# Spreading a block's rounds of weight sums over its attention units, and mixing one quarter later

## The chip, the cores and the metric

The kernel runs on one core of a Trainium2 chip. The metric is the time of one execution on the device in microseconds (us); the median of several runs counts. The core's engines work side by side, each through its own list of instructions in order: TensorE (PE, with its weight loads PEld), VectorE (DVE), ScalarE (ACT), GpSimd (POOL) and SyncE (SP). They wait for one another through semaphores.

## The reference, cut to what matters

2048 tokens (32 sequences of 64, 1024 wide) pass a grouped attention and a linear layer with adapters. All is float32.

```python
mixed = einsum('bct,bcd->bdt', x, W_mix[itok])        # one 64x64 matrix per sequence: "mixing"
q, k, v = mixed @ Wq.T, mixed @ Wk.T, mixed @ Wv.T    # 32 heads of 128 for q, 8 for k and v
q, k = rmsnorm(q) * q_norm_w, rmsnorm(k) * k_norm_w
attn = softmax(q @ k.T / sqrt(128) + alibi_bias)      # causal, 64x64 per sequence and head
x = x + (attn @ v) @ Wo.T                             # output projection
x = x + ffn(base_and_low_rank(x))                     # linear in x, folded into one 1024x1024 matrix
```

## The kernel before

**Tiling.** The tokens are worked in four blocks of 512, each of four tiles of 128 tokens. A block is a list of units: `kv` (keys and values of two key heads), `q` (queries of one key head's four heads, with their attention), `o` and `p` (output projection of a pair of key heads) and `f` (the last linear layer, two halves). `units()` gives the order: kv q q kv o q q kv o q q kv o q q p o f f. A kv, q or f unit has four steps, one for each tile; a step is four **quarters**, each of six 128x512 matmuls (each product is made of three, of the upper and lower parts of both factors, so that float32 is kept). A block has 336 quarters. In block 0 the first pair of q units spans quarters 16 to 48, the first projection `o` 64 to 92, the next two q units 92 to 124, the second projection 140 to 168, the q units behind it 168 to 200, the third projection 216 to 236.

**The order.** It is written out by `Order` before the program is built. `at(base, delay, work)` puts work at a position in quarters; `tick` steps from quarter to quarter and takes all work whose position has been reached, in order of position. Every engine then goes through the same list and takes its own stages. Delays of stages behind a step stand in `AT`; those of the keys' transposes in `KEYS_AT` (transpose on PE, k_hi on ACT, k_lo on DVE), where "mixing" is for the first three steps of a block's first kv unit in blocks 1 to 3. A q step runs: four quarters of matmuls, square (ACT), mean (DVE), rstd (POOL), scale (DVE), query_t (PE), q_hi (ACT), q_lo (DVE), scores (PE), alibied, biased, peak (DVE), exp (ACT), total, inverse, prob (DVE), transpose (PE), p_hi, p_twice (ACT), p_lo (DVE), the product with the values (PE).

**Weights.** Each quarter's weights are loaded by SP into one of four raw buffers; w_hi (ACT) and w_lo (DVE, 128x1024) split them into one of six slots of a ring, when the slot's former chunk is done. So four w_lo come together at the end of a kv or q unit: at 30.6, 32.6, 33.6 and 35.6 for the unit that ends at quarter 32, and at the same places of the other units.

**Weights' sums.** The projection is done by seven products of sums instead of eight (`OPS`), so it needs four sums of the quarters of `Wo` for each of eight rounds (pair, c). A round (`sums_load`, `sums_add`, `sums_store`) is four t_load of 512 KB on POOL, four additions t1 to t4 of 128x1024 on DVE (7.2, 8.7, 10.2 and 11.7 quarters after the round's start) and four t_store on POOL (at 12.8), into `t_scratch`, from where later units fetch them as weights through SP. Three rounds run in the setup, five in block 0 at `ROUND_AT`. Their buffers lie in `lefts`, the left factors of the projections; so each round has to be done before a projection in block 0 needs them (`ROUND_BEFORE`, a wait in op_hi), and a round must not start while one runs.

**Mixing.** `f_step` of the second f unit loads the next block's tile of x (`reload`, on POOL), splits it (`mix_split`: x_hi on ACT, x_lo on DVE) and mixes it (`mix`: 16 matmuls into four banks, four a_hi on ACT, four a_rest and four a_lo on DVE, written as act_lo). The tile at step i of the f unit ends its step at quarter 324 + 4i of its block, and is needed by the next block's first kv unit at quarter 336 + 4i.

Of the kernel before, what the change touches and what calls it, by code (L numbers as in the profile page):

```python
# [19 lines left out]
HEADS, KV_HEADS, HD = 32, 8, 128  # L20
# [25 lines left out]
          tp=7.9, tp_hi=8, tp_again=9.2, tp_lo=8.6,  # L46
          v=10.6, v_hi=11.5,
          add=1.6,
          mix_split=7.4, mix=9.8, reload=5.1,
          x1=2.2, low=4.6, low_end=6.0, out=0.6, c22=0.2,  # L50
          w_hi=0.3, w_lo=0.9)

KEYS_AT = dict(mixing=(2.8, 3.4, 3.9), queries=(3.8, 4.4, 4.9), projection=(4.8, 5.4, 5.9))
LATE = dict(s=0.5, s_add=0.5, s_exp=0.5, s_norm=0.5, tp=1.2, tp_hi=1.2, tp_again=1.2, tp_lo=1.2, v=1.6, v_hi=1.6)


# [5 lines left out]
OPS = (("11", "11", "a"), ("s3", "t3", "d"), ("12", "21", "a"), ("s2", "t2", "b"),  # L65
       ("s1", "t1", "e"), ("22", "t4", "b"), ("s4", "22", "e"))
# [10 lines left out]
QUARTERS = 4  # L77
# [7 lines left out]
SETUP_ROUNDS = 3  # L85

WARM = 22, 8
ROUND_AT = (0.5, 18.5, 35, 104, 180)

ROUND_BEFORE = (2, 1), (3, 0), (3, 1), (3, 1)  # L90

PART_OF = [(n + 2) % TILES for n in range(KT + 1)]

# [13 lines left out]
def ops_of(unit):  # L107


    kind, blk, pair = unit  # L110
    if kind == "p":
        return 4, 6
    return (0, 1, 2, 3, 5) if pair == 2 else range(len(OPS))


def tiles_of(blk):

    return (0, 1, 2, 3) if blk % 2 == 0 else (2, 3, 0, 1)


def is_o(unit):
    return unit[0] in ("o", "p")
# [71 lines left out]
class Order(Plan):  # L194
# [249 lines left out]
    def blocks(self):  # L444

        self.at(0, 14, lambda: self.add("fx_store"))
        for n in range(SLOTS, len(self.chunks)):
            self.at(self.prepared_at[n], 0, self.prepare)
        for (pair, c), start in zip(ROUNDS[SETUP_ROUNDS:], ROUND_AT):
            self.at(start, 0, lambda pair=pair, c=c: self.sums_load(pair, c))  # L450

            wait = 3.5 if start < QUARTERS else 0
            for i, stage in enumerate(("t1", "t2", "t3", "t4")):
                self.at(start, wait + 7.2 + 1.5 * i, lambda pair=pair, c=c, stage=stage: self.sums_add(pair, c, [stage]))
            self.at(start, wait + 12.8, lambda pair=pair, c=c: self.sums_store(pair, c))
        for u, unit in enumerate(self.units):
            if unit[0] == "o":
                self.left_factors(unit)
            elif unit[0] == "p":

                for tp in range(2):
                    self.at(QUARTERS * self.first_step[unit], tp - 2.9, lambda unit=unit, tp=tp: self.kept_sum(unit[1], unit[2], tp))
        for k, (u, i) in enumerate(self.steps):
            kind, blk, n = self.units[u]
            if k in (0, 1):
                self.later(FIRST_MIX[k], lambda k=k: self.mix(0, k + 2))
            if kind == "kv":
                self.kv_step(k)
            elif kind == "q":
                self.q_step(k, n, tiles_of(blk)[i])  # L470
            elif is_o(self.units[u]):
                self.o_step(k, blk, n, ops_of(self.units[u])[i])
            else:
                self.f_step(k, blk, n, tiles_of(blk + 1)[i])
        while self.side:
            self.tick()
# [44 lines left out]
    def kv_step(self, k):  # L521
# [7 lines left out]
        else:  # L529
            place = "projection" if i == TILES - 1 else "queries"  # L530
        transposed, upper, lower = KEYS_AT[place]

# [191 lines left out]
def build_program(nc, d, out):  # L724
# [3 lines left out]
    with ctx:  # L728
# [193 lines left out]
        def o_step(blk, pair, m):  # L922
            return order.op[blk, pair, m]
# [321 lines left out]
        def _(eng):  # L1245
# [10 lines left out]
            for stage, key in order.stages:  # L1256
# [180 lines left out]
                elif stage == "op_hi":  # L1437
# [12 lines left out]
                    if blk == 0:  # L1450
                        for i in range(4):
                            w.wait_ge(f"t_store{i}", *ROUND_BEFORE[pair])
                    w.wait_ge("mix_mm", blk, tiles_of(blk)[2], len(MIX_BANKS) - 1)
# [363 lines left out]
        @block.gpsimd  # L1817
        def _(eng):
            w = Waits(eng, order, done)
            for stage, key in order.stages:  # L1820
                if stage == "mixw_zero":
                    eng.memset(mixw_raw[:, :, :], 0.0).then_inc(done[stage], 1)
                elif stage == "half_set":
                    eng.memset(half[:, :], -0.5).then_inc(done[stage], 1)
                elif stage == "ones_set":
                    eng.memset(prob[:, :], 1.0).then_inc(done[stage], 1)
                elif stage.startswith("f_store"):
                    n, u = key
                    w.wait_ge("f_copy", n, u)
                    eng.dma_start(f_scratch[u, n // 2, :, n % 2, :], stage_tile(order.copies[n, u][0])).then_inc(done[stage], 16)  # L1830
                elif stage in ("x0", "x1", "x2", "x3"):
                    blk, = key
                    t = int(stage[1])
                    if blk > 0:
                        w.wait_ge(f"out{t}", blk - 1)
                    elif t < 2:
                        left, of = order.first_tiles[t]
                        w.wait_ge(left, *of)
                    else:
                        for left, of in order.stage_left:  # L1840
                            w.wait_ge(left, *of)
                    eng.dma_start(acc[:, t, :], d["x"][blk * TILES + t]).then_inc(done[stage], 16)
                elif stage == "rstd":
                    k, = key
                    heads = norm_width(k)
                    w.wait_ge("mean", k)
                    w.wait_ge("half_set")
                    if earlier_norm(k, 1) is not None:
                        w.wait_ge("scale", earlier_norm(k, 1))
                    eng.tensor_tensor(rstd[:, 0:heads], mean[:, 0:heads], half[:, 0:heads], ALU.pow).then_inc(done[stage], 1)  # L1850
                elif stage.startswith("t_load"):
                    pair, c = key
                    i = int(stage[-1])
                    n = ROUNDS.index(key)
                    if n == 0:
                        w.wait_ge("coef_masked")
                    elif n == SETUP_ROUNDS:

                        w.wait_ge("weff_mm", KT, 1, 3)
                        w.wait_ge("w_hi", SLOTS - 1)  # L1860
                    else:
                        w.wait_ge(f"t_store{i}", *ROUNDS[n - 1])
                    if pair == KV_HEADS // 2 - 1:
                        w.wait_ge("mm", o_step(0, c, len(OPS) - 1), 3)
                    eng.dma_start(sums_of(pair, c)[i][:, :], d["wo"][pair, i, c]).then_inc(done[stage], 16)
                elif stage.startswith("t_store"):
                    pair, c = key
                    i = int(stage[-1])
                    name = next(t for t in SUM_AT if SUM_AT[t] == i)
                    w.wait_ge(name, pair, c)  # L1870
                    eng.dma_start(t_scratch[pair, int(name[1]) - 1, c], sums_of(pair, c)[i][:, :]).then_inc(done[stage], 16)
                elif stage in ("fx_load0", "fx_load1"):
                    blk, = key
                    i = 2 * int(stage[-1])
                    last = KV_HEADS // 2 - 1
                    w.wait_ge("fx_store")
                    w.wait_ge("s4", blk, last)
                    w.wait_ge("op_lo", o_step(blk, last, 4 if i == 0 else 6))
                    eng.dma_start(extra[:, i:i + 2, :], extra_scratch[:, i:i + 2, :]).then_inc(done[stage], 16)
                elif stage == "biased_x":  # L1880
                    blk, t = key
                    w.wait_ge("a_lo", "x1", blk, t | 1, 1)
                    w.wait_ge("bias_add", 1)
                    eng.tensor_tensor(acc[:, t, :], acc[:, t, :], bias_eff[:, :], ALU.add).then_inc(done[stage], 1)
                elif stage.startswith("out"):
                    blk, = key
                    t = int(stage[3])
                    f_k = order.first_step["f", blk, 1] + tiles_of(blk + 1).index(t)
                    w.wait_ge("acc", f_k, 1)
                    eng.dma_start(out[blk * TILES + t], acc[:, t, :]).then_inc(done[stage], 16)  # L1890
            for t in range(TILES):
                w.wait_ge(f"out{t}", BLOCKS - 1)
            for left, of in order.stage_left:
                w.wait_ge(left, *of)
            eng.memset(half[:, :], -0.5).then_inc(done["half_set"], 1)
# [92 lines left out]
```

## Time and profile before

| | us |
|---|---|
| Median of three runs (lowest, highest) | 2375.29 (2374.58, 2379.8) |
| Profiled execution, own time | 2375.95 |
| its span | 2374.0 |
| PE busy | 2344.8 |
| DVE busy | 1776.3 |
| ACT busy | 1464.5 |
| POOL busy | 285.1 |

The main loop starts 136.6 us after the span's start and ends at 2360.1; what stands ahead of it is the setup. Busy PE is counted from modelled ends of pipelined matmuls, so a wait shorter than a matmul's tail doesn't show as idle time; the distance from the start of one group of matmuls to the next shows it. "Granted clock" is the share of TensorE's full clock that the chip grants.

### The profile page before, as it was taken

The numbers are of one execution on the slowest core, as the hardware profiler recorded it, in microseconds if no ns is written. First come the engines' busy times: TensorE is split into PE (matmuls) and PEld (weight loads), VectorE is DVE, ScalarE is ACT, GpSimd is POOL, SyncE is SP. The second block draws the span as 40 slices with busy tenths as digits, with TensorE's granted clock in tenths as the row PEclk, the third lists the DMA queues.
The fourth block names the chain that finished last, engine by engine and source line by source line (L and its number), as shares of the span: only waits on it lengthen the run. The fifth ranks groups of instructions, "written<-read, shape, count | busy, mean of one in ns | idle before, by whom it ended". The sixth has DMA issues, their size and how long they took to land.

```text
span 2374.0 us, 33429 instructions
## 1 busy us (share of the span) xinstructions
PE 2344.8 (99%) x11706; PEld 1961.6 (83%) x11706; DVE 1776.3 (75%) x2930; ACT 1464.5 (62%) x3625; POOL 285.1 (12%) x336
## 2 busy tenths in 40 slices
PE   8999999999999999999999999999999999999998
PEld 6877888888888888888888888888888888888886
DVE  6777969696847878787846777777876696969691
ACT  4246767576625857576824857576844676767660
POOL 1222010101011001010021101010021101010111
PEclk9999999999999999999999999999999999999999
DMA  6774434442542242423443242423244242423250
GB/s 254 265 262 187 160 134 155 147 135 73 195 150 89 86 145 74 148 72 134 143 153 116 72 160 71 160 72 124 97 172 144 81 150 70 151 80 139 73 197 36
DMA packets 88440, 316.16 MB, mean 133 GB/s; under 512 B 12716, under 2 KB 13228, under 8 KB 87124
## 3 DMA queue, kind: packets, MB, share of 16 engines
q1 hardware_dynamic: 70292, 247.14, 30.1%
q0 software_dynamic: 16256, 62.92, 7.2%
q10 hardware_dynamic: 1728, 3.98, 0.5%
q8 instruction: 95, 1.56, 0.3%
q14 instruction: 69, 0.57, 0.1%
HBM read 282.54 MB, written 31.46 MB: 132 GB/s over the span
## 4 chain that ended last, share of the span: by engine, by line
PE 94%; DVE 3%; DMA 1%; issue 1%; ACT 0%; POOL 0%; ACTq 0%; POOLq 0%; DVEq 0%
PE main L1041 80%; PE qt_bank L1202 3%; PE s_bank L1218 3%; PE s_bank L1219 2%; PE pv_bank L1239 1%; PE pv_bank L1238 1%; PE pt_bank L1226 1%; PE pt_bank L1041 1%; DVE ring L1511 1%; DVE setup L1511 0%; PE qt_bank L1139 0%; PE s_bank L1139 0%; DMA acc<-in_x 0%; DMA t_scratch<-sums 0%; DMA mask<-in_masks 0%
## 5 line engine op out<-in xcount | busy, mean ns | idle before, releaser
L1041 PE MATMUL main<-ring,act_hi 128*128 128x512 f32 x3584 | 1148.4, 402 | 0.4 <-DVE ring L1511 0.3
L1041 PEld LDWEIGHTS main<-ring,act_hi 128*128 128x128 f32 x3584 | 641.5, 189 | 114.3 <-issue 3.1
L1041 PE MATMUL main<-ring,act_lo 128*128 128x512 f32 x1792 | 701.7, 392 | 0.0
L1041 PE MATMUL main<-ring,lefts 128*128 128x512 f32 x2688 | 625.9, 391 | 0.0
L1041 PEld LDWEIGHTS main<-ring,lefts 128*128 128x128 f32 x2688 | 499.9, 188 | 101.5
L1511 DVE TENSOR_TENSOR ring<-raw,ring 128x1024 fp32r<-128x1024 f32 x448 | 550.5, 1233 | 41.1 <-ACT ring L1249 38.9
L1249 ACT ACTIVATE ring<-raw 128x1024 fp32r<-128x1024 f32 x448 | 472.0, 1056 | 172.0 <-PE main L1041 149.6
L1041 PEld LDWEIGHTS main<-ring,act_lo 128*128 128x128 f32 x1792 | 336.9, 188 | 74.9
L1850 POOL TENSOR_TENSOR rstd<-mean,half 128x4 f32<-128x4 f32 (+1 forms) x192 | 174.0, 906 | 1535.1 <-DVE mean L1636 1535.0
L1382 ACT ACTIVATE sq<-main 128x128 f32<-128x128 f32 x640 | 169.3, 277 | 76.1 <-PE main L1041 72.2
L1410 ACT ACTIVATE prob<-score,peak 128x64 f32<-128x64 f32 x512 | 136.1, 336 | 98.1 <-DVE peak L1694 97.4
L1514 DVE TENSOR_TENSOR acc<-main,acc 128x512 f32<-128x512 f32 x164 | 112.2, 685 | 87.2 <-PE main L1041 87.1
L1249 ACT ACTIVATE qt_hi<-qt_bank 128x512 fp32r<-128x512 f32 x128 | 76.6, 598 | 126.8 <-PE qt_bank L1202 124.9
L1715 DVE TENSOR_TENSOR pt_lo<-pt_bank,pt_hi 64x256 fp32r<-64x256 f32 x256 | 107.7, 421 | 59.2 <-ACT pt_hi L1420 57.5
L1420 ACT ACTIVATE pt_hi<-pt_bank 64x256 fp32r<-64x256 f32 x256 | 96.9, 379 | 66.8 <-PE pt_bank L1226 65.3
L1511 DVE TENSOR_TENSOR lefts<-quads,lefts 128x1024 fp32r<-128x1024 f32 x112 | 136.5, 1219 | 0.5
L1249 ACT ACTIVATE lefts<-quads 128x1024 fp32r<-128x1024 f32 x112 | 118.3, 1056 | 25.9 <-PE main L1041 23.4
L1656 DVE TENSOR_TENSOR qn<-main,rstd 128x512 f32<-128x512 f32 (+1 forms) x192 | 114.5, 596 | 25.7 <-POOL rstd L1850 24.2
L1382 ACT ACTIVATION_READ_ACCUMULATOR sq<-main 128x1 f32 x640 | 131.6, 206 | 0.0
L1511 DVE TENSOR_TENSOR qt_lo<-qt_bank,qt_hi 128x512 fp32r<-128x512 f32 x128 | 88.0, 688 | 57.4 <-ACT qt_hi L1249 57.4
L1219 PE MATMUL s_bank<-k_t,qt_lo 128*128 128x64 f32 x512 | 117.3, 245 | 0.0
L1218 PE MATMUL s_bank<-k_t,qt_hi 128*128 128x128 f32 x512 | 115.1, 286 | 1.2 <-issue 1.2
(168 smaller groups left out, 2554.3 us busy)
## 6 DMA issues: line engine op xcount, KB each, us to landing
raw<-in_wq SPq DMA_DIRECT2D x128, 512.0 KB, 4.3
raw<-t_scratch SPq DMA_DIRECT2D x128, 512.0 KB, 3.2
raw<-in_wo SPq DMA_DIRECT2D x96, 512.0 KB, 3.2
raw<-in_wkv SPq DMA_DIRECT2D x64, 512.0 KB, 3.9
sums<-in_wo POOLq DMA_DIRECT2D x32, 512.0 KB, 7.6
t_scratch<-sums POOLq DMA_DIRECT2D x32, 512.0 KB, 4.1
raw<-f_scratch SPq DMA_DIRECT2D x32, 512.0 KB, 4.9
acc<-in_x POOLq DMA_DIRECT2D x16, 512.0 KB, 4.1
```

What stands on the lines that cost most here:

```text
L1041: mm = eng.matmul(bank, a, b, start=start and n == 0 and m == 0, stop=stop and n == len(terms) - 1 and m == 2, skip_group_check=further)
L1218: eng.matmul(s_bank[:, a:a + 2 * SEQ], lh, keys, start=True, stop=False)
L1219: mm = eng.matmul(s_bank[:, a:a + SEQ], ll, keys[:, 0:SEQ], start=False, stop=True)
L1249: eng.activation(dst, src, ACT.Copy).then_inc(done[stage], 1)
L1382: act = eng.activation(sq[:, tile(h)], norm_bank(k)[:, tile(h)], ACT.Square, accum_out=ssum[:, h:h + 1])
L1410: act = eng.activation(prob[:, cols], score[:, cols], ACT.Exp, bias=peak[:, r:r + 1], scale=-1.0)
L1420: act = eng.activation(pt_hi[rows_of(b), b, :], pt_bank[rows_of(b), 0:256], ACT.Copy)
L1511: eng.tensor_tensor(dst, src, f32(upper), ALU.subtract).then_inc(done[stage], 1)
L1514: eng.tensor_tensor(dst, a, b, ALU.add).then_inc(done[stage], 1)
L1656: eng.tensor_tensor(heads_of(norm_tile(k)[:, cols], heads), heads_of(norm_bank(k)[:, cols], heads), along(rstd[:, 0:heads], heads), ALU.mu ...
L1715: rest = eng.tensor_tensor(pt_lo[rows_of(b), b, :], pt_bank[rows_of(b), 0:256], f32(pt_hi[rows_of(b), b, :]), ALU.subtract)
L1850: eng.tensor_tensor(rstd[:, 0:heads], mean[:, 0:heads], half[:, 0:heads], ALU.pow).then_inc(done[stage], 1)
```

## The change

Five things are edited. The five rounds of block 0 start at 24, 95, 111.5, 171 and 187.5 quarters instead of 0.5, 18.5, 35, 104 and 180. `ROUND_BEFORE` follows: the first projection waits for round (1,1), the second for (2,1), the third and fourth for (3,1). The extra 3.5 quarters that the round of the first quarters had are dropped. The t_loads of both rounds of pair 2 and of pair 3 wait for the end of the projection two pairs earlier (0 or 1); before, only those of pair 3 waited, each for another projection. And at the edges of blocks the split moves from 7.4 to 8.4 and the mixing from 9.8 to 10.5, with the keys of the "mixing" steps from 2.8, 3.4, 3.9 to 3.8, 4.35, 4.38.

```diff
@@ AT
-          mix_split=7.4, mix=9.8, reload=5.1,
+          mix_split=8.4, mix=10.5, reload=5.1,
@@
-KEYS_AT = dict(mixing=(2.8, 3.4, 3.9), queries=(3.8, 4.4, 4.9), projection=(4.8, 5.4, 5.9))
+KEYS_AT = dict(mixing=(3.8, 4.35, 4.38), queries=(3.8, 4.4, 4.9), projection=(4.8, 5.4, 5.9))
@@
-ROUND_AT = (0.5, 18.5, 35, 104, 180)
-
-ROUND_BEFORE = (2, 1), (3, 0), (3, 1), (3, 1)
+ROUND_AT = (24, 95, 111.5, 171, 187.5)
+
+ROUND_BEFORE = (1, 1), (2, 1), (3, 1), (3, 1)
@@ blocks
             self.at(start, 0, lambda pair=pair, c=c: self.sums_load(pair, c))
-
-            wait = 3.5 if start < QUARTERS else 0
             for i, stage in enumerate(("t1", "t2", "t3", "t4")):
-                self.at(start, wait + 7.2 + 1.5 * i, lambda pair=pair, c=c, stage=stage: self.sums_add(pair, c, [stage]))
-            self.at(start, wait + 12.8, lambda pair=pair, c=c: self.sums_store(pair, c))
+                self.at(start, 7.2 + 1.5 * i, lambda pair=pair, c=c, stage=stage: self.sums_add(pair, c, [stage]))
+            self.at(start, 12.8, lambda pair=pair, c=c: self.sums_store(pair, c))
@@ gpsimd, t_load
-                    if pair == KV_HEADS // 2 - 1:
-                        w.wait_ge("mm", o_step(0, c, len(OPS) - 1), 3)
+                    if pair >= 2:
+                        w.wait_ge("mm", o_step(0, pair - 2, len(OPS) - 1), 3)
```

## Rows read from the trace of the kernel before

**Rows 1.** The page: busy time of PE, and the chain by engine

```profile
PE 2344.8 (99%) x11706; PEld 1961.6 (83%) x11706; DVE 1776.3 (75%) x2930; ACT 1464.5 (62%) x3625; POOL 285.1 (12%) x336
...
PE 94%; DVE 3%; DMA 1%; issue 1%; ACT 0%; POOL 0%; ACTq 0%; POOLq 0%; DVEq 0%
```

**Rows 2.** Windows: stretch, length, busy by engine (instructions), granted clock, DMA share, GB/s

```profile
136.60:703.20 566.60, 557.59 (x2776) 464.55 (x2777) 435.71 (x715) 358.40 (x894) 79.93 (x100) 0.99 0.44 158
703.20:1256.40 553.20, 553.20 (x2794) 465.23 (x2793) 418.30 (x702) 356.50 (x893) 60.29 (x62) 1.00 0.35 119
...
136.60:153.50 16.90, 15.99 (x82) 12.88 (x83) 15.95 (x27) 10.76 (x22) 2.82 (x5) 1.00 0.88 314
```

**Rows 3.** Timeline, second tile of block 2: start us, us, instruction; PE, then DVE

```profile
1259.09 0.28 PE L1125 MATMUL qt_bank<-mixw,x_odd 128*128 128x256 f32 x1
...
1260.88 0.68 PE L1041 MATMUL main<-ring,act_hi 128*128 128x512 f32 x2
...
1262.32 0.62 PE L1041 MATMUL main<-ring,act_hi 128*128 128x512 f32 x2
...
1263.81 0.70 PE L1041 MATMUL main<-ring,act_hi 128*128 128x512 f32 x2
...
1263.24 0.43 DVE L1514 TENSOR_TENSOR act_lo<-pv_bank,act_lo 128x256 fp32r<-128x256 f32 x1
```

**Rows 4.** PE's waits in blocks 1 to 3 (total, times, longest); ACT's timeline, block 2

```profile
PE qt_bank L1125 <- DVE k_t L1511: 0.7, 1, 0.7
...
1272.33 1.06 ACT L1249 ACTIVATE x_odd<-acc 128x1024 fp32r<-128x1024 f32 x1 [3.34 <-DMA acc<-in_x]
```

**Rows 5.** PE's waits in block 0: total us, times, longest

```profile
PE qt_bank L1202 <- DVE qn L1656: 6.0, 4, 4.1
...
PE qt_bank L1202 <- DVE qn L1663: 0.7, 1, 0.7
```

**Rows 6.** POOL's timeline around its wait; landing of all t_stores (source view, L1871)

```profile
167.02 1.06 POOL L1871 DMA_DIRECT2D t_scratch<-sums  x2 [1.16 <-DVE sums L1775]
...
177.67 0.53 POOL L1865 DMA_DIRECT2D sums<-in_wo  x1 [3.54 <-DMA t_scratch<-sums]
178.22 1.04 POOL L1850 TENSOR_TENSOR rstd<-mean,half 128x4 f32<-128x4 f32 x1
...
DMA to landing us min/median/max: 3.0/4.1/9.8
```

**Rows 7.** Windows, columns as in rows 2, behind that wait

```profile
178.60:185.40 6.80, 5.36 (x15) 4.39 (x16) 1.55 (x3) 1.74 (x9) 0.88 (x2) 0.50 0.69 281
```

**Rows 8.** Timeline at the round of quarter 35: DVE, then PE

```profile
231.34 1.22 DVE L1775 TENSOR_TENSOR sums<-sums,sums 128x1024 f32<-128x1024 f32 x1
232.48 0.68 DVE L1511 TENSOR_TENSOR qt_lo<-qt_bank,qt_hi 128x512 fp32r<-128x512 f32 x1
...
229.00 0.60 PE L1202 MATMUL qt_bank<-ident,qn 128*128 128x128 f32 x4
...
233.26 0.30 PE L1218 MATMUL s_bank<-k_t,qt_hi 128*128 128x128 f32 x1 [0.66 <-issue]
...
238.42 0.66 PE L1202 MATMUL qt_bank<-ident,qn 128*128 128x128 f32 x4 [0.79 <-DVE qn L1656]
```

**Rows 9.** PE timeline, same place of block 1, without a round

```profile
755.86 0.60 PE L1202 MATMUL qt_bank<-ident,qn 128*128 128x128 f32 x4
...
759.29 0.22 PE L1218 MATMUL s_bank<-k_t,qt_hi 128*128 128x128 f32 x1
...
763.53 0.66 PE L1202 MATMUL qt_bank<-ident,qn 128*128 128x128 f32 x4
```

**Rows 10.** Timeline, first tile of block 2: PE, then DVE

```profile
1251.09 0.28 PE L1125 MATMUL qt_bank<-mixw,lefts 128*128 128x256 f32 x1
...
1252.11 0.42 DVE L1511 TENSOR_TENSOR act_lo<-qt_bank,act_hi 128x256 fp32r<-128x256 f32 x1 [2.85 <-ACT act_hi L1249]
...
1254.94 0.42 DVE L1514 TENSOR_TENSOR act_lo<-pv_bank,act_lo 128x256 fp32r<-128x256 f32 x1
```

## The prediction

> **What bounds the kernel now.** I read the page's busy shares and its chain first: TensorE (PE) is busy 99% of the span and carries 94% of the chain [rows 1]. PE runs one written-out order of 1344 quarters (six 128x512 matmuls each; 1.36 us from start to start in the median), so time is lost only where PE waits in that order. Next I cut the trace at the first matmul of each block of tokens [rows 2]: block 0 takes 566.6 us, block 1 takes 553.2. Block 0 also mixes one tile less (1.79 us, 1259.09 to 1260.88 [rows 3]), so it loses 15.2 us that block 1 doesn't. Its first eight quarters with two mixings lose 2.2 of them: 16.9 us [rows 2] against 8 x 1.36 + 2 x 1.8 + 0.14 for a transpose = 14.7; nothing that the change moves stands there for PE. The other 13.0 us are, as far as the trace tells, what the rounds of weights' sums cost. Blocks 1 to 3 have no round, and one PE wait of note, 0.7 us, with some 0.5 behind it [rows 4]. So there are 13 us to win from in block 0, and 1.2 us at the block edges.
>
> **Part 1: where the 13 us sit.** Round (2,0) follows round (1,1) too soon. Its t_loads wait on GpSimd (POOL) for the t_stores of the round before, POOL takes its work in order, and behind them stands rstd, which scale and query_t need. POOL waits 3.54 us for the last store, issues the load at 177.67 and rstd only at 178.22 [rows 6]. PE waits 4.1 us for that scale [rows 5], and the granted clock then is 0.50 for 6.8 us [rows 7]; PE restarts at 180.0, so 5.4 us run at half rate, 2.7 us more. With 0.7 us for the key transpose behind the round's additions [rows 5], that is 7.5 us. The other 5.5 are VectorE's (DVE's) backlog at the five rounds.
>
> **The change removes that POOL wait.** Round (1,1) starts at 24 with no store just ahead of it. Rounds (2,0) and (3,0), at 95 and 171, wait for a projection that ends at quarter 92 or 168, and POOL's next rstd is due at 97.3 and 173.3. Rounds (2,1) and (3,1) start 16.5 quarters after their forerunners. From stores to the rstd behind the loads that leaves 5.5 quarters (107.8 to 113.3), 10.5 us at the 1.92 us that a quarter takes here (755.86 to 763.53 are four [rows 9]); a store lands 4.1 us after its issue in the median and 9.8 at most [rows 6]. Before, it was 4.5 short quarters (16.8 to 21.3), 6 to 7 us. So I cost the wait at nothing, at most 1 us. The five rounds still issue the same 20 loads, 20 stores and 20 additions; on SP nothing moves, since the results are fetched a projection later.
>
> **What the rounds cost on DVE in their new places.** Each addition takes a slot of 1.14 us on DVE (231.34 to 232.48 [rows 8]), in a stretch where four w_lo of the next weights take as much each within five quarters. The round at 35 shows the price. t4 stands ahead of q_lo, and the scores start at 233.26; the next query_t, behind its scale, at 238.42 [rows 8]. Without a round, query_t to scores takes 3.43 us and scores to query_t 4.24 [rows 9]; from the query_t at 229.00 the scores would come at 232.43, and the next query_t 4.24 after 233.26, at 237.50. So 0.83 + 0.92 = 1.8 us. t1 to t3 fall into gaps of DVE.
> - 95 and 171 stand at the same place of their unit (3 quarters in) as 35: 1.8 each.
> - 111.5 and 187.5 are half a quarter further on: t3 falls ahead of a scale (0.5), t4 ahead of q_lo (0.6), and the backlog reaches the next scale (0.9): 2.0 each.
> - 24 is the worst place. Its additions stand at 31.2, 32.7, 34.2, 35.7 and the w_lo at 30.6, 32.6, 33.6, 35.6. Laid into block 1's order [rows 9] at 1.14 us each: the scores come 0.2 late, the next query_t 2.1 (two additions ahead of its scale), the transpose of the probabilities 0.1, the next scores 1.4 (t3 and t4 ahead of q_lo): 3.8 us.
>
> Sum 1.8 + 1.8 + 2.0 + 2.0 + 3.8 = 11.4 us against 13.0: part 1 **gains 1.6 us**. Bounds: with each round at 0.8 (all but the last of its slots hidden) a gain of 9; with a half clock at the first round a loss of 1.
>
> On the clock, the rows show a fall after 4.1 us of waiting [rows 5, 7] and none after 0.8 [rows 8]. The Trainium skill, "TensorE: Matmul & The Clock Gate", section on the HAM clock gate, says that idleness of PE throttles the array to half (here 2.4 to 1.2 GHz) and activity frees it. The trace agrees; if the rule already takes the waits of 2.1 and 1.4 us at round (1,1) for idleness, the sum is that of the first rival below.
>
> **Part 2: the mixing.** An action at a position that is no whole quarter is taken at the next whole one. A mixing at 9.8 goes into PE's order two quarters ahead of the step that needs its tile; at 10.5 only one. So all 12 mixings for blocks 1 to 3 move by a whole quarter, not 0.7. Behind a mixing hangs a chain that can't shrink: four act_hi on ScalarE (ACT), eight act_lo on DVE, and the kv step's first matmul waits for the last of them. At the second tile of block 2 the mixing starts at 1259.09, the next quarters at 1260.88 and 1262.32, the step that needs the tile at 1263.81; its last act_lo starts at 1263.24 and takes 0.43, so PE starts 0.14 behind it [rows 3]: **the slack is already nil**. The chain by itself: the first act_lo 1.02 us after the mixing starts, the last ends at 1255.37, 4.28 us after it [rows 10]. One quarter later, PE has 1.79 (mixing) + 1.44 (one quarter) = 3.23 us of work from the mixing's start; it then waits 4.28 + 0.14 - 3.23 = 1.19, less 0.13 that it waits now (1262.32 to 1263.81 is 1.49, a quarter 1.36): **1.06 us a tile**. For the third and fourth tile a key transpose (0.14) fills some of it: 1.0 each. The first tile's cover is a quarter of nine matmuls (1.5 x 1.36 + 0.08 = 2.12, the 0.08 for following a mixing: 1.44 less 1.36): 4.42 - 3.91 = 0.5. One block edge: 0.5 + 1.06 + 1.0 + 1.0 = 3.6 us; three edges 10.8. The later split (8.4) and keys (3.8) don't lengthen the chain: laid out the same way, x_lo, mean, v_lo, scale and gain are through DVE before each chain's first act_lo, by 0.1 to 0.6 us. Where they are not, a tile costs up to 1.5.
>
> **What it gives back.** In block 2 the last tile's mixing waits on k_lo, since x_hi, held up 3.34 us by a late x tile, stands ahead of k_hi on ACT [rows 4]. With k_hi at 4.35 ahead of the split at 4.4, this goes: 1.2 us. Bounds of part 2: a loss of 8 to 14, less 1.2.
>
> **Sum.** -1.6 + 10.8 - 1.2 = +8.0 us. The profiled execution took 2375.95 us with a span of 2374.0, 0.7 us over the median of 2375.29; such a difference is noise, and I add to the median: **2383.3 us**, 0.34% slower.
>
> **Rivals.**
> - *The clock falls at round (1,1)*, after waits of 2.1 and 1.4 us within 7: another 2.7 us, 2386.0. 8%.
> - *The new places are nearly free*: all 13 us go but for 5 x 0.8, so -9.0 + 9.6 = +0.6: 2375.9, no change. For it: t1 to t3 of the round at 35 are free. Against: the w_lo stand just there, and the same count of slots reproduces the 1.8 us measured at 35. 10%.
> - *Faster: the kv step doesn't wait for the chain.* If the last act_lo came within 3.23 us of the mixing's start rather than 4.28, the later mixing would be hidden: -1.6 - 1.2, 2372.5, and 2365 if the new places are cheap as well. Against: eight DVE operations without a gap fill 3.26 us alone (1252.11 to 1255.37 [rows 10]), and 0.14 us between act_lo and matmul [rows 3] is a wait that just ended. 4%.
> - *The move is less than I read* (positions rounded otherwise): mixings cost half or nothing, 2373 to 2379. 4%.
>
> **How the numbers follow.** Forecast 74%: 2383.3. What a measurement can tell from no change is about 0.2%, 4.75 us: faster is under 2370.5, slower over 2380.0. The clock's rival is slower; the forecast is slower but for its lower end (cheaper rounds, about a tenth of it, with little lost at the edges); the cheap places and the smaller move are mostly same; the faster rival is shared between same and faster. Faster 0.03, same 0.15, slower 0.82. For 8 in 10 the range takes the forecast with its bounds and the clock's rival: 2378 to 2389.
>
> **What would show it.** Right: no POOL wait for t_scratch that holds an rstd, clock 1.00 through block 0, a query_t near quarter 34 that waits about 2 us for its scale, and at each block edge PE waits of about 1 us for act_lo ahead of kv steps. Wrong: kv steps that start on time after a mixing one quarter later; a first round without its wait of 2 us, or with a half clock; or new waits for t_scratch, x tiles or weights.

## The result, and the profile after

| | before | changed |
|---|---|---|
| median of six runs each, us (lowest to highest) | 2376.61 (2374.58 to 2379.8) | 2386.01 (2385.59 to 2386.99) |
| ratio of the runs' times (95% interval) | | 1.0039 (1.0026 to 1.0052) |
| span of the profiled execution, us | 2374.0 | 2384.4 |

The change costs 9.4 us by the medians and 10.4 us by the two profiled spans. The forecast was 2383.3 with a range of 2378 to 2389, and slower at 0.82. The new runs of the kernel before put its median 1.3 us above the one the forecast was added to; so the forecast rise of 8.0 us stands against 9.4 and 10.4. The spans are those of one profiled execution each, and the runs of the kernel before range over 5.2 us, those of the changed kernel over 1.4.

The page of the changed kernel, busy time of the engines and the chain by engine (compare [rows 1]):

```profile
PE 2345.0 (98%) x11706; PEld 1960.6 (82%) x11706; DVE 1772.8 (74%) x2930; ACT 1465.1 (61%) x3625; POOL 285.2 (12%) x336
...
PE 91%; DVE 6%; issue 1%; ACT 1%; DMA 0%; POOL 0%; ACTq 0%; POOLq 0%; DVEq 0%
```

The instructions and PE's busy time are the same; the chain has moved from PE (94% to 91%) to DVE (3% to 6%). PE stands still more, and what it stands still for is DVE.

The blocks, as windows of the changed kernel (stretch, length, busy by engine, granted clock, DMA share, GB/s; compare [rows 2]):

```profile
136.30:700.50 564.20, 554.64 (x2777) 462.84 (x2777) 435.08 (x715) 357.75 (x894) 80.08 (x100) 1.00 0.46 158
700.50:1258.70 558.20, 554.31 (x2793) 465.07 (x2793) 416.31 (x702) 356.63 (x894) 60.30 (x62) 1.00 0.36 118
1258.70:1816.90 558.20, 554.33 (x2792) 465.06 (x2793) 416.42 (x702) 356.69 (x894) 60.22 (x62) 1.00 0.36 118
1816.90:2370.40 553.50, 550.01 (x2768) 461.85 (x2769) 411.14 (x689) 348.02 (x882) 58.70 (x59) 1.00 0.33 110
```

Block 0 went from 566.6 to 564.2 us, and its clock from 0.99 to 1.00; block 1 from 553.2 to 558.2. Blocks 2 and 3 took 554.4 and 549.3 before. So the differences are -2.4, +5.0, +3.8 and +4.2 us, with -0.3 for the setup: 10.3 of the span's 10.4. The first tile's loss at the first edge (some 0.6 us) falls ahead of the cut, into block 0, so the rounds, all in block 0, gained about 3; the edges of blocks lost a lot.

The waits of PE in blocks 1 to 3 of the changed kernel (total us, times, longest):

```profile
PE main L1039 <- DVE act_lo L1512: 7.9, 9, 1.0
PE qt_bank L1200 <- DVE qn L1661: 2.6, 3, 0.9
PE main L1039 <- issue: 1.2, 3, 0.4
```

Before, only 0.7 us of waiting stood out there [rows 4]. The nine waits for act_lo are the second to fourth tile of each of three edges, and the three called "issue" the first tiles: these twelve were forecast. The three waits for qn, one at each edge, were not.

**The edge, seen closely.** The second tile of block 2, PE and then DVE (start us, us; idle time ahead of it in brackets), answers to [rows 3]:

```profile
1262.90 0.28 PE L1123 MATMUL qt_bank<-mixw,x_odd 128*128 128x256 f32 x1
...
1264.69 0.68 PE L1039 MATMUL main<-ring,act_hi 128*128 128x512 f32 x2
...
1267.32 0.47 PE L1039 MATMUL main<-ring,act_hi 128*128 128x512 f32 x1 [1.02 <-DVE act_lo L1512]
...
1266.75 0.42 DVE L1512 TENSOR_TENSOR act_lo<-pv_bank,act_lo 128x256 fp32r<-128x256 f32 x1
```

Now only one quarter lies between the mixing and the step that needs its tile. From that quarter's start to the step's it is 1267.32 - 1264.69 = 2.63 us; a quarter there takes 1.44, and 0.13 was waited before, so the tile costs 2.63 - 1.44 - 0.13 = 1.06 us.

**The wait for the store is gone.** POOL's timeline at the stores of round (2,0), the one at 95, and the loads of round (2,1):

```profile
318.12 1.06 POOL L1869 DMA_DIRECT2D t_scratch<-sums  x2 [3.98 <-DVE sums L1773]
...
324.00 0.53 POOL L1863 DMA_DIRECT2D sums<-in_wo  x1 [0.74 <-DMA t_scratch<-sums]
...
328.21 1.03 POOL L1848 TENSOR_TENSOR rstd<-mean,half 128x4 f32<-128x4 f32 x1 [3.69 <-DVE mean L1634]
```

A load still waits 0.74 us for its store (1.1 at the other such place), but POOL is idle again for 3.69 us before the next rstd asks for it. In [rows 6] the rstd came right behind the load.

**The round at 24.** PE, with DVE under it:

```profile
192.23 0.30 PE L1216 MATMUL s_bank<-k_t,qt_hi 128*128 128x128 f32 x1
...
198.52 0.66 PE L1200 MATMUL qt_bank<-ident,qn 128*128 128x128 f32 x4 [1.92 <-DVE qn L1654]
...
203.57 0.30 PE L1216 MATMUL s_bank<-k_t,qt_hi 128*128 128x128 f32 x1 [1.09 <-issue]
...
190.31 1.22 DVE L1762 TENSOR_TENSOR sums<-sums,sums 128x1024 f32<-128x1024 f32 x1
...
194.06 1.23 DVE L1766 TENSOR_TENSOR sums<-sums,sums 128x1024 f32<-128x1024 f32 x1
...
196.65 1.21 DVE L1509 TENSOR_TENSOR ring<-raw,ring 128x1024 fp32r<-128x1024 f32 x1
197.78 0.68 DVE L1654 TENSOR_TENSOR qn<-main,rstd 128x512 f32<-128x512 f32 x1
```

Two additions (190.31, 194.06) and the w_lo lie ahead of the scale at 197.78, and DVE has no gap between 189.18 and there. Scores to query_t take 198.52 - 192.23 = 6.29 us, where 4.24 is usual [rows 9]: 2.05 lost. Query_t to scores take 5.05 against 3.43: 1.62. With 0.2 for the scores at 192.23, which are late themselves, that is 3.9 us.

### The profile page after: what moved, and what is told of

It is laid out like the page before. It is cut to its first block, busy times and chain, and to the rows that moved or that the text cites. A ratio compares the mean times of both kernels' runs of the same rounds, so it can differ in the third digit from the quotient of the medians.

```text
span 2384.4 us, 33429 instructions
## 1 busy us (share of the span) xinstructions
PE 2345.0 (98%) x11706; PEld 1960.6 (82%) x11706; DVE 1772.8 (74%) x2930; ACT 1465.1 (61%) x3625; POOL 285.2 (12%) x336
## 4 chain that ended last, share of the span: by engine, by line
PE 91%; DVE 6%; issue 1%; ACT 1%; DMA 0%; POOL 0%; ACTq 0%; POOLq 0%; DVEq 0%
PE main L1039 79%; PE qt_bank L1200 3%; PE s_bank L1216 2%; PE s_bank L1217 2%; PE pv_bank L1237 1%; PE pt_bank L1224 1%; PE pv_bank L1236 1%; DVE ring L1509 1%; PE pt_bank L1039 1%; DVE act_lo L1509 1%; DVE act_lo L1512 1%; PE s_bank L1137 0%; DVE qn L1654 0%; DVE setup L1509 0%; PE qt_bank L1137 0%
## 5 line engine op out<-in xcount | busy, mean ns | idle before, releaser
L1039 PEld LDWEIGHTS main<-ring,act_hi 128*128 128x128 f32 x3584 | 640.4, 189 | 124.4 <-issue 13.5
```

Source lines behind the costliest of these rows:

```text
L1039: mm = eng.matmul(bank, a, b, start=start and n == 0 and m == 0, stop=stop and n == len(terms) - 1 and m == 2, skip_group_check=further)
```

## The experiments

The theory so far: the new places of the rounds are worth a little (POOL's wait goes, DVE's backlog stays), and the loss is the mixing's whole quarter. The rivals still open: that the rounds' new places do more or less than that and the edges' part differs by as much; that the keys or the split, not the mixing, lengthen the edges; and, for the first round, that its price is not set by the w_lo beside it. In what follows a cost of some quarters is the sum of the distances from the start of one group of matmuls to the next, less the median distance of the same kind of group in the trace of the kernel before.

**e1: the rounds alone.** Mixing, split and keys stay as before.

```diff
-ROUND_AT = (0.5, 18.5, 35, 104, 180)
-ROUND_BEFORE = (2, 1), (3, 0), (3, 1), (3, 1)
+ROUND_AT = (24, 95, 111.5, 171, 187.5)
+ROUND_BEFORE = (1, 1), (2, 1), (3, 1), (3, 1)
...
-            wait = 3.5 if start < QUARTERS else 0
...
-                    if pair == KV_HEADS // 2 - 1:
-                        w.wait_ge("mm", o_step(0, c, len(OPS) - 1), 3)
+                    if pair >= 2:
+                        w.wait_ge("mm", o_step(0, pair - 2, len(OPS) - 1), 3)
```

> The new places of the rounds alone, with mixing, split and keys as before. Theory A (trace accounting): the wait on POOL and the half clock go (about 7.5 us), the five additions' backlog costs 10 to 11 us in the new places against 13 in all before: 2 to 3.5 us faster than before, clock 1.00 through block 0, block 0 564 us long. Rival B (the slowdown comes from the rounds, too): no gain, or slower than before by some us.

Measured: 2374.73 us against 2376.74 of the kernel before beside it, ratio 0.9992 (0.9983 to 1.0001); the span is 2371.3, 2.7 below that before. So the rounds' new places are a gain of 2 to 3 us, on the edge of what the runs can tell from none. Block 0 is 563.5 us long, as was expected, but its clock was not 1.00 throughout: see the rivals further down.

**e2: the edges alone.** Split, mixing and keys as in the change, the rounds as before.

```diff
-          mix_split=7.4, mix=9.8, reload=5.1,
+          mix_split=8.4, mix=10.5, reload=5.1,
...
-KEYS_AT = dict(mixing=(2.8, 3.4, 3.9), queries=(3.8, 4.4, 4.9), projection=(4.8, 5.4, 5.9))
+KEYS_AT = dict(mixing=(3.8, 4.35, 4.38), queries=(3.8, 4.4, 4.9), projection=(4.8, 5.4, 5.9))
```

> The later mixing, split and keys alone, rounds as before. Theory A: 12 to 14 us slower than before (four waits at each of three block edges, about 4.8 us an edge, 1.2 us given back in block 2); with the rounds-alone kernel it adds up to the whole change. Rival B (the two halves interact): the sum of both differs from the whole change by over 2 us.

Measured: 2389.62 us, ratio 1.0051 (1.0037 to 1.0065), span 2386.1: 12.1 us over the span before. Windows of e2, blocks 0 and 1, columns as above:

```profile
136.70:702.90 566.20, 557.53 (x2776) 464.45 (x2776) 434.77 (x715) 357.46 (x894) 79.78 (x100) 0.99 0.45 158
702.90:1260.70 557.80, 553.87 (x2792) 465.20 (x2793) 418.39 (x702) 356.35 (x894) 60.21 (x62) 1.00 0.35 118
```

Block 0 keeps its 0.99 and its length; block 1 has the length of the changed kernel's. The two halves add up: -2.7 + 12.1 = 9.4 in spans against 10.4 for the whole, and -2.0 + 12.9 = 10.9 in medians against 9.4. The edges alone are more than the 9.6 of the forecast, so something is in them beside the mixing.

**e3: the mixing alone**, split and keys as before.

```diff
-          mix_split=7.4, mix=9.8, reload=5.1,
+          mix_split=7.4, mix=10.5, reload=5.1,
```

> Only the mixing's position moves, 9.8 to 10.5, split and keys as before. Theory A (the chain of act_lo is the cost, as in the prediction): 3.6 us an edge, 9.5 to 11 us slower than before, and no wait of PE for gain at the fourth key transpose. Rival B (the keys and the split carry most of the loss): under 6 us slower.

**e4: the keys alone.**

```diff
-KEYS_AT = dict(mixing=(2.8, 3.4, 3.9), queries=(3.8, 4.4, 4.9), projection=(4.8, 5.4, 5.9))
+KEYS_AT = dict(mixing=(3.8, 4.35, 4.38), queries=(3.8, 4.4, 4.9), projection=(4.8, 5.4, 5.9))
```

> Only the keys of the block edges' first three kv steps move (2.8, 3.4, 3.9 to 3.8, 4.35, 4.38); mixing and split as before. The prediction's step: no cost. Theory A, from the trace of the changed kernel (k_lo of the third step stands ahead of w_lo on DVE and now waits 3.3 us for its transpose; the gain of the fourth step comes 1 us late): 1.0 to 1.2 us an edge, 3 to 3.5 us slower than before. Rival B (prediction): within 0.5 us of before.

Measured: e3 2386.46 us, ratio 1.0038 (1.0024 to 1.0051); e4 2380.33 us, ratio 1.0015 (1.0006 to 1.0024). PE's waits in blocks 1 to 3, e3 and then e4:

```profile
PE main L1041 <- DVE act_lo L1514: 6.5, 9, 1.0
PE main L1041 <- issue: 1.2, 3, 0.4
```

```profile
PE qt_bank L1202 <- DVE qn L1663: 2.5, 3, 0.8
PE main L1041 <- DVE act_lo L1514: 1.0, 2, 0.7
```

The twelve waits of the mixing belong to e3, the three for qn to e4: two causes, each with its own edit. The two waits for act_lo in e4, 0.3 and 0.7 us, come within 1.1 us behind the x_hi of a late x tile; e5 and e8, whose keys aren't moved, have one such wait each (0.4 and 0.5). e3 plus e4 is 9.7 + 3.6 = 13.3 us by the medians, against 12.9 for e2. The traces say the same: from the last scores ahead of an edge to the first behind it, summed over the three edges, e3 loses 9.9 us against the kernel before, e4 4.1 and the changed kernel 13.5. The same sum for e5 and e8, whose edges are in effect as before, is +0.9 and -0.2, so it is good to about 1 us. The keys were costed at nothing. The split (8.4) wasn't run alone; e2 less e3 and e4 leaves it -0.4 us, which is nothing that these runs can tell.

How the keys cost it. The step before the one that waits, on DVE, changed kernel, block 2:

```profile
1287.52 1.22 DVE L1509 TENSOR_TENSOR ring<-raw,ring 128x1024 fp32r<-128x1024 f32 x1
1292.06 0.42 DVE L1509 TENSOR_TENSOR k_t<-qt_bank,k_t 128x256 fp32r<-128x256 f32 x1 [3.32 <-ACT k_t L1247]
1292.40 1.22 DVE L1509 TENSOR_TENSOR ring<-raw,ring 128x1024 fp32r<-128x1024 f32 x1
...
1296.33 0.43 DVE L1661 TENSOR_TENSOR qn<-qn,kgain 128x256 f32<-128x256 f32 x1
...
1296.81 0.44 PE L1200 MATMUL qt_bank<-ident,qn 128*128 128x128 f32 x2 [0.85 <-DVE qn L1661]
```

The same k_lo in the kernel before, and then in e4:

```profile
1285.31 0.42 DVE L1511 TENSOR_TENSOR k_t<-qt_bank,k_t 128x256 fp32r<-128x256 f32 x1 [0.53 <-ACT k_t L1249]
```

```profile
1288.03 0.42 DVE L1511 TENSOR_TENSOR k_t<-qt_bank,k_t 128x256 fp32r<-128x256 f32 x1 [2.26 <-ACT k_t L1249]
```

The third step's k_lo has moved behind a transpose that PE does a quarter later, but in DVE's order it still stands ahead of w_lo. DVE idles 3.32 us for it (before 0.53), and the w_lo that it could have done in that time come behind: the fourth step's gain at 1296.33 has one w_lo right behind k_lo (1292.40) and another between its mean and scale. It ends late by what PE waits, 0.85 us and some tail, about 1.2 us at each edge, 3.5 in all.

**e5: how a position is rounded.** Mixing from 9.8 to 10.0 only, which is the same whole quarter.

```diff
-          mix_split=7.4, mix=9.8, reload=5.1,
+          mix_split=7.4, mix=10.0, reload=5.1,
```

> Only the mixing's position moves, 9.8 to 10.0: 0.2 of the change's 0.7 quarter, but the same whole quarter. Theory A (positions are taken at the next whole quarter, and the cost comes with the whole quarter): no change from before, within 1 us. Rival B (the cost goes with the distance moved): 2/7 of the mixing's loss, about 3 us slower.

Measured: a median of 2377.37 us against 2375.31 beside it, 2.1 us apart; the ratio of the runs' times is 1.0003 (0.9994 to 1.0012), that is from 1.4 us less to 2.9 us more. By time alone that leaves the rival's 3 us only just out, so the trace has to say it. PE's waits in e5 (total us, times, longest):

```profile
PE qt_bank L1202 <- DVE qn L1656: 7.8, 4, 5.9
...
PE main L1041 <- DVE act_lo L1514: 0.4, 1, 0.4
```

e3 has nine waits for act_lo, 6.5 us; e5 has one, 0.4 us, and its block 1 is 554.0 us long (553.2 before, 557.0 in e3). The span is 2.6 us over that of before, and 1.8 of them are POOL's wait in block 0, which this edit doesn't touch: PE waits 5.9 us there instead of 4.1. So what matters of the change's 0.7 quarter is the step from 10.0 to 10.5, that is one whole quarter; the rival "the move is less than I read" is out.

**e6: the first round off the w_lo.** In the changed kernel, the round at 24 starts at 19; its additions then stand at 26.2 to 30.7, and the first w_lo at 30.6.

```diff
-ROUND_AT = (24, 95, 111.5, 171, 187.5)
+ROUND_AT = (19, 95, 111.5, 171, 187.5)
```

> The changed kernel with round (1,1) at 19 instead of 24, so that it stands in its unit as the round at 35 did before. Theory A (a round's price is the count of its additions among the four w_lo): the 3.9 us at quarters 32 to 39 become 1.8, 2.1 us faster than the changed kernel, and the query_t wait of 1.9 us near quarter 34 falls to about 0.9. Rival B (the price is the transfers' or any round's own): as the changed kernel.

Measured: 2384.92 us, ratio 1.0037 (1.0023 to 1.005), span 2381.7 against 2384.4 of the changed kernel. The wait rows of PE around that round (total us, times, longest):

```profile
PE qt_bank L1200 <- DVE qn L1654: 0.8, 1, 0.8
PE s_bank L1216 <- issue: 0.7, 1, 0.7
```

And its block 0, as a window:

```profile
136.10:698.30 562.20, 554.18 (x2776) 462.98 (x2777) 434.88 (x715) 357.76 (x894) 79.92 (x100) 1.00 0.46 159
```

Of the waits of 1.92 and 1.09 us 0.8 and 0.7 are left, quarters 32 to 39 lose 2.6 instead of 4.7, and block 0 is 2.0 us shorter. The same 4 additions cost about half as much when they don't share their quarters with four w_lo. By the medians alone (2384.92 and 2386.01, intervals of the ratios that overlap) the 2 us can't be told; it is the place in the trace that shows it.

**e7: the second round closer to the first.** In the changed kernel, the round at 111.5 starts at 109: 1.2 quarters behind the stores instead of 3.7.

```diff
-ROUND_AT = (24, 95, 111.5, 171, 187.5)
+ROUND_AT = (24, 95, 109, 171, 187.5)
```

> The changed kernel with round (2,1) at 109 instead of 111.5: its t_loads stand on POOL ahead of the rstd at 109.3, one and a half quarters behind the stores of round (2,0) that they wait for. Theory A (the t_loads' wait for stores blocks the rstd behind it): a POOL wait for t_scratch of 2 to 5 us and a PE wait of 1 to 4 us for scale near quarter 110; the round's own additions cost less there (1.4 us gone). Together 0 to 3 us slower than the changed kernel. Rival B (POOL's wait is harmless): 1.4 us faster than the changed kernel.

Measured: 2390.26 us, ratio 1.0059 (1.0045 to 1.0073), span 2388.7, 4.3 over the changed kernel's. POOL's timeline, and PE's:

```profile
323.32 0.53 POOL L1863 DMA_DIRECT2D sums<-in_wo  x1 [1.72 <-DMA t_scratch<-sums]
...
325.31 0.53 POOL L1863 DMA_DIRECT2D sums<-in_wo  x1 [1.46 <-DMA t_scratch<-sums]
325.85 1.03 POOL L1848 TENSOR_TENSOR rstd<-mean,half 128x4 f32<-128x4 f32 x1
...
327.66 0.66 PE L1200 MATMUL qt_bank<-ident,qn 128*128 128x128 f32 x4 [3.41 <-DVE qn L1654]
```

The window behind that wait:

```profile
329.00:332.40 3.40, 3.40 (x11) 2.60 (x10) 2.18 (x4) 2.12 (x10) 0.00 (x0) 0.50 1.02 413
```

This is [rows 6] and [rows 7] again, in another unit: loads wait for stores, rstd stands right behind them, PE waits 3.41 us for the scale, and the granted clock is 0.50 behind it. So this wait and not the number of rounds or their place in the first quarters is what the change took away; it comes back as soon as a round follows its forerunner too closely. Block 0 is 568.0 us, 3.8 over the changed kernel's. That is more than the 0 to 3 us expected. Some 1.4 us are lost ahead of the round's place, in the setup and the first quarters, where the two kernels have the same order; at the round itself e7 loses 3.4 all told, and the expectation had no half clock in it.

**e8: both causes taken away.** The changed kernel with the old split, mixing and keys, and every round placed so that its additions fall between two groups of w_lo: at 33, 93, 109.5, 169 and 185.5.

```diff
-          mix_split=8.4, mix=10.5, reload=5.1,
+          mix_split=7.4, mix=9.8, reload=5.1,
...
-KEYS_AT = dict(mixing=(3.8, 4.35, 4.38), queries=(3.8, 4.4, 4.9), projection=(4.8, 5.4, 5.9))
+KEYS_AT = dict(mixing=(2.8, 3.4, 3.9), queries=(3.8, 4.4, 4.9), projection=(4.8, 5.4, 5.9))
...
-ROUND_AT = (24, 95, 111.5, 171, 187.5)
+ROUND_AT = (33, 93, 109.5, 169, 185.5)
```

> The rounds at 33, 93, 109.5, 169 and 185.5, mixing, split and keys as before: each round's four additions then end before the first w_lo of its unit. Theory A: each round costs under 0.5 us, block 0 loses 2 to 4 us in all against 13 for the rounds before: 10 to 12 us faster than the kernel before, about 2365. Rival B (an addition costs its 1.14 us slot wherever it stands): 5 x 1.8 or more, 1 to 4 us faster.

Measured: 2368.54 us against 2375.31, ratio 0.9971 (0.9959 to 0.9983), span 2365.5: 6.8 us faster than before by the medians, and faster than both kernels. The largest of PE's waits in block 0:

```profile
PE qt_bank L1200 <- DVE qn L1654: 3.6, 7, 0.7
```

The windows of blocks 0 and 1:

```profile
136.50:695.00 558.50, 553.86 (x2776) 463.19 (x2777) 435.78 (x715) 358.26 (x894) 79.71 (x100) 1.00 0.46 160
695.00:1248.30 553.30, 553.30 (x2793) 465.25 (x2793) 416.09 (x702) 356.48 (x893) 60.26 (x62) 1.00 0.36 119
```

Block 0 is 8.1 us shorter than before (566.6), block 1 is as before (553.2). But seven waits for a scale are left, 3.6 us, and some tails: the rounds still cost 13.0 - 8.1 = 4.9 us, 1.0 each, where the expectation had under 0.5. So it missed its 10 to 12 us; its rival (1 to 4 us, every addition at its full slot) is out as well. One of the seven, on DVE, at the second addition of the round at 93:

```profile
302.58 1.22 DVE L1766 TENSOR_TENSOR sums<-sums,sums 128x1024 f32<-128x1024 f32 x1
303.71 0.68 DVE L1654 TENSOR_TENSOR qn<-main,rstd 128x512 f32<-128x512 f32 x1
```

An addition that shares its quarters with no w_lo can still stand right ahead of a scale; PE waits 0.33 us for this one.

## Why the prediction was right, and where it was off

**The base.** 1.3 us of the difference between forecast and median is the kernel before, whose median of six is 2376.61 and of three was 2375.29. The rest is best read in spans, where one profile stands against the other: forecast +8.0, measured +10.4. (8 x 1.36 + 2 x 1.8 + 0.14 is 14.6, not 14.7, so the rounds' 13.0 us should read 12.9; nothing hangs on it.)

**POOL's wait goes: right.** At most 1 us was allowed for it; the loads wait 0.74 and 1.1 us with POOL idle for 3.7 us behind them, so it costs nothing. The clock is 1.00 in block 0. e7 shows the mechanism by bringing it back.

**What the rounds cost in their new places: right in kind, 1.1 us too dear.** Forecast and measured (quarters around the round, over the same quarters of block 0 without one):

| round at | forecast, us | measured, us |
|---|---|---|
| 24 | 3.8 | 3.9 |
| 95 | 1.8 | 1.8 |
| 111.5 | 2.0 | 1.4 |
| 171 | 1.8 | 1.8 |
| 187.5 | 2.0 | 1.4 |
| sum | 11.4 | 10.3 |

The term that was mis-sized is the 0.5 us for t3 ahead of a scale in the rounds at 111.5 and 187.5. The changed kernel's timeline at 111.5:

```profile
344.52 1.21 DVE L1769 TENSOR_TENSOR sums<-sums,sums 128x1024 f32<-128x1024 f32 x1
345.65 0.68 DVE L1654 TENSOR_TENSOR qn<-main,rstd 128x512 f32<-128x512 f32 x1
...
342.26 0.22 PE L1216 MATMUL s_bank<-k_t,qt_hi 128*128 128x128 f32 x1
...
346.39 0.65 PE L1200 MATMUL qt_bank<-ident,qn 128*128 128x128 f32 x4
...
350.31 0.30 PE L1216 MATMUL s_bank<-k_t,qt_hi 128*128 128x128 f32 x1 [0.25 <-issue]
...
355.46 0.66 PE L1200 MATMUL qt_bank<-ident,qn 128*128 128x128 f32 x4 [0.81 <-DVE qn L1654]
```

t3 does stand right ahead of the scale, but query_t comes 4.13 us after the scores, no later than without a round (4.24 in [rows 9]): the scale had that much slack. Behind t4 it goes as forecast: 3.92 against 3.43 and 5.15 against 4.24, 0.5 + 0.9 = 1.4. So the rounds gain 13.0 - 10.3 = 2.7 us and not 1.6; e1's span says 2.7 too.

**The mixing's quarter: right.** Forecast 0.5, 1.06, 1.0 and 1.0 us for an edge's four tiles; measured 0.6 to 0.7, 1.06 and about 1.0 for each of the last two. At the first edge, counted from the last scores ahead of it, the fourth step starts 3.7 us later than in the kernel before, in the changed kernel and in e3 alike. With the give-back, forecast 10.8 - 1.2 = 9.6; e3's edges lose 9.9. That an action counts from the next whole quarter on is what e5 shows.

**The give-back: not settled.** No mixing waits behind a late x tile in the changed kernel. But none does in e3 either, where the keys and the split stand as before, and none in e8, whose edges are those of the kernel before. Which block has the wait, and how long it is, differs between runs of the old order: 0.7 us in block 2 [rows 4], 0.2 in e5, and in e1 1.3 us in block 1. So the reason given, k_hi ahead of the split, isn't shown. What does go with the mixing's later quarter is ACT's wait for late x tiles: 5.6 to 7.9 us over the three edges in the five kernels with the mixing at 9.8 or 10.0, and 0.5 us at most in the five with 10.5. The runs of the first five (6 to 21 each) range over 4.5 to 7.4 us, those of the second five (5 or 6 each) over 1.4 to 2.8; that the x tiles are the reason isn't shown.

```profile
PE qt_bank L1123 <- DVE k_t L1509: 1.3, 1, 1.3
```

**The step that failed.** "The later split (8.4) and keys (3.8) don't lengthen the chain: ... x_lo, mean, v_lo, scale and gain are through DVE before each chain's first act_lo". That was laid out for the mixing's chain, and for that it held (the fourth step of an edge comes no later than in e3). What it left out is what stands behind the moved k_lo in DVE's own order: w_lo, and then the next step's mean, scale and gain for the key transpose. The third step's key has no mixing behind it to hide an idle DVE. It costs 3.5 us over three edges (e4 alone: +3.6 by the medians). It was the "what is queued behind the waiting instruction" question, asked of POOL and not of DVE.

In spans: 8.0 - 1.1 (rounds) + 3.5 (keys) = 10.4 us, the measured one. The terms of the edges are known to about 1 us, so that this comes out to the tenth is luck. And the two errors partly cancel: the keys alone would have put the time 3.5 us off.

**The rivals.** The clock's rival put the fall at round (1,1), with another 2.7 us. In the changed kernel the clock stayed at 1.00 there. In e1, whose round (1,1) is the same, it did fall, behind the same 1.92 us wait. PE's timeline in e1, and the window behind it:

```profile
198.57 0.74 PE L1200 MATMUL qt_bank<-ident,qn 128*128 128x128 f32 x4 [1.92 <-DVE qn L1654]
```

```profile
199.00:202.40 3.40, 3.40 (x12) 2.71 (x10) 3.33 (x6) 1.15 (x3) 1.13 (x2) 0.50 0.78 295
```

It lasted 3.4 us, and it cost nothing: quarters 32 to 39 lose 4.73 us in e1 and 4.72 in the changed kernel (against medians; 0.8 of it is lost there without a round as well, which leaves the 3.9 of the table). DVE was the one behind, so PE at half its rate (1.2 GHz) only used up time that it would else have waited for the next q_lo. The rival's price was wrong, its possibility not. "The new places are nearly free" is out for these places (10.3 us against its 4), though e8's places come near it. "Faster, since the kv step doesn't wait for the chain" is out by 1.06 us a tile.

## What to carry to other kernels

When an operation is moved later in a written-out order, look up what stands behind it on its own engine, and whether its input moves by more than it does: the engine idles for it, and the work it could have done then comes due later in front of something PE waits for. A chain of eight small operations between two matmuls can't be given less than its own length, here 4.28 us; a stage that is moved by 0.7 of a quarter may go by a whole one. And extra work on a helper engine costs by what shares its quarters, not by its amount: the same five rounds cost 10.3 us in the changed kernel's places and 4.9 in e8's. In the old places they cost 13.0, but 6.8 of these were POOL's wait and the half clock behind it; for DVE alone the old places were cheaper than the changed kernel's.

## What the runs showed of the hardware

The granted clock fell to 0.50 at waits of PE of 4.1 us [rows 5, 7] and 3.41 us (e7), for 6.8 and 3.4 us. What the forecast gave only 8% is that a wait of 1.92 us can do it: it did in e1 (3.4 us long), and in another run of the same stretch it didn't (changed kernel, 1.00 throughout block 0). The Trainium skill, "TensorE: Matmul & The Clock Gate", section on the HAM clock gate, has idleness throttle the array. These traces agree with that, and add that the length of a single wait alone doesn't decide it. The kernels that keep the old rounds bear it out: at waits of 3.6, 4.3 and 5.9 us (e2, e3, e5) the clock was 0.50 for 6.8 us, at one of 4.0 us (e4) for 3.4. And a half clock is only worth its price where PE is what the others wait for: 2.7 us were worked out for the kernel before, none was found in e1.
